# Combining matmuls cut into column tiles, and new positions for the steps around them, in a two-layer cross-attention and mixture-of-experts kernel

## The reference

```
x = x + cross_attention_0(layernorm(x), ctx)          # 16 heads of 8, all 1601 keys
x = x + experts_0(layernorm(x))                       # top 2 of 9, inner width 352
x = x + cross_attention_1(layernorm(x), ctx, indices) # 16 heads of 8, 64 chosen keys per query
x = x + experts_1(layernorm(x))                       # top 2 of 8, and a shared one, inner width 176
```

## Time and profile before

| | us |
|---|---|
| median of 3 runs | 1537.95 |
| lowest, highest | 1526.84, 1542.74 |
| the profiled execution's own time | 1533.95 |
| its span, first to last instruction | 1531.8 |
| PE, DVE, ACT, POOL busy | 1395.9, 1092.1, 789.7, 828.1 |

### The profile page before, as it was taken

One profiled execution on the slowest core, in us unless ns is written; L12 is line 12 of the kernel. 1 busy time (PEld: TensorE's weight loads), 2 busy tenths in 40 slices (PEclk: granted clock), 3 DMA queues, 4 the chain that ended last, 5 costly groups with the idle time before them and its releaser, 6 DMA issues.

```text
span 1531.8 us, 34069 instructions
## 1 busy us (share of the span) xinstructions
PE 1395.9 (91%) x12588; PEld 804.0 (52%) x12588; DVE 1092.1 (71%) x2283; ACT 789.7 (52%) x1200; POOL 828.1 (54%) x1381
## 2 busy tenths in 40 slices
PE   4899799999999999999999999999999999997987
PEld 2244464357533674347743575346843477334845
DVE  4885578866787668877688667876588776865663
ACT  3457337652575426772376524764266723773451
POOL 4356346755566545664457544675456644544462
PEclk8799899999998999999999999999999999997997
DMA  4505310132102330023201421023300331000111
GB/s 111 144 22 150 81 48 12 30 100 66 34 19 49 90 82 2 22 78 86 55 2 34 96 74 36 12 67 79 83 2 23 77 89 26 1 7 28 41 41 45
DMA packets 97654, 82.12 MB, mean 54 GB/s; under 512 B 17658, under 2 KB 90644, under 8 KB 97492
## 3 DMA queue, kind: packets, MB, share of 16 engines
q1 hardware_dynamic: 96916, 78.72, 19.8%
q10 hardware_dynamic: 576, 1.23, 0.3%
HBM read 67.29 MB, written 12.61 MB: 52 GB/s over the span
## 4 chain that ended last, share of the span: by engine, by line
PE 63%; DVE 20%; ACT 5%; POOL 5%; issue 4%; DMA 1%; SPq 0%; ACTq 0%; POOLq 0%; DVEq 0%
PE ob L788 10%; PE um L846 8%; PE ob L863 7%; DVE mx L1259 7%; PE um L847 7%; PE um L773 6%; PE um L758 6%; PE um L736 4%; ACT probs L1054 2%; DVE mx L1376 2%; DVE big L1372 2%; DVE xn L1157 2%; PE um L830 2%; PE um L913 2%; PE um L730 1%
## 5 line engine op out<-in xcount | busy, mean ns | idle before, releaser
L1259 DVE TENSOR_REDUCE mx<-um 128x2 f32<-128x802 f32 (+1 forms) x512 | 501.6, 989 | 177.3 <-PE um L758 173.6
L1054 ACT ACTIVATE probs<-um 128x1024 f32<-128x1024 f32 (+1 forms) x448 | 425.7, 963 | 215.2 <-PE um L773 211.0
L1452 POOL TENSOR_TENSOR hid<-hid,cwb 128x256 f32<-128x256 f32 (+1 forms) x304 | 217.0, 732 | 265.3 <-DVE hid L1271 130.2
L1060 ACT ACTIVATE hid<-um 128x256 f32<-128x256 f32 (+1 forms) x304 | 116.7, 384 | 346.0 <-PE um L847 336.8
L1458 POOL TENSOR_TENSOR big<-iotab,idx_lo 128x512 bf16<-128x512 bf16 x256 | 272.0, 1078 | 28.3 <-PE um L953 20.4
L788 PE MATMUL ob<-probs,vaug 128*9 128x256 f32 (+1 forms) x3328 | 280.6, 386 | 3.2 <-ACT oT L1035 2.7
L758 PE MATMUL um<-kst,qa 64*128 64x401 bf16 (+1 forms) x1024 | 178.4, 347 | 25.3 <-DMA kst<-k_parts 9.8
L773 PE MATMUL um<-big,kst 64*128 64x256 bf16 (+1 forms) x1664 | 171.1, 280 | 14.5 <-DVE mx L1376 4.8
L1271 DVE TENSOR_TENSOR hid<-hid,um 128x256 f32<-128x256 f32 (+1 forms) x304 | 124.4, 414 | 55.8 <-ACT hid L1060 53.0
L846 PE MATMUL um<-xnT,w1T 128*128 128x256 f32 (+1 forms) x400 | 129.3, 406 | 0.0
L863 PE MATMUL ob<-w2T,hid 128*128 128x128 f32 (+1 forms) x800 | 124.2, 280 | 4.6 <-POOL hid L1452 3.7
(11 more groups left out here) (221 smaller groups left out, 2087.9 us busy)
## 6 DMA issues: line engine op xcount, KB each, us to landing
kst<-k_parts SPq DMA_DIRECT2D x360, 50.0 KB
cwb<-cw_rows SPq DMA_DIRECT2D x112, 128.0 KB, 3.4
k_parts<-big SPq DMA_DIRECT2D x72, 128.0 KB, 1.9
ctx_sb<-in_ctx SPq DMA_DIRECT2D x7, 768.0 KB
cwb<-cw_rows SPq DMA_DIRECT2D x48, 96.0 KB, 3.0
k1st<-k_parts SPq DMA_DIRECT2D x96, 32.0 KB
cwb<-cw_rows SPq DMA_DIRECT2D x48, 64.0 KB, 2.7
cwb<-cw_rows SPq DMA_DIRECT2D x16, 112.0 KB, 3.0
```

The lines of the kernel that those rows point to most:

```text
L1054: act.activation(probs[0:kn, k:k + 2, 0:w], own_banks, ACT.Exp).then_inc(f_read, 1)
L1060: act.activation(hid[0:nr, own % NHID, :], quarter[place[ev][0]][0:nr, 0:NQ], ACT.Silu).then_inc(th_ready, 1)
L1259: dve.tensor_reduce(mx[:, p % 2, s, :, j], pair[:, :, 0:w], AX, ALU.max, negate=True).then_inc(u_read, 1)
L1452: pool.tensor_tensor(h, h, cwb[0:nr, k, :], ALU.mult).then_inc(hw_ready, 1)
```

## The change

Each half of 128 queries is combined in four products of 32 queries. The stationary operand is 32 columns of oT, the output goes to partitions 32t to 32t + 31, and the product stands in the column tile of that position. The numbers computed are the same. The positions change too: 42 of the 123 constants of AT, and SHIFT has 142 entries where it had 19.

```diff
             def combine(bank, o):
 
                 for s in range(NS):
-                    m = pe.matmul(bank[:, s * 2 * V1:(s + 1) * 2 * V1], o[:, s * P:(s + 1) * P], comb[:, :], start=True, stop=True)
+                    for t in range(P // QD):
+                        m = pe.matmul(bank[QD * t:QD * (t + 1), s * 2 * V1:(s + 1) * 2 * V1], o[:, s * P + QD * t:s * P + QD * (t + 1)],
+                                      comb[:, :], start=True, stop=True, tile_position=(0, QD * t))
                 return m
```

Of the tables AT and SHIFT, some of the entries that differ:

```diff
-'c0': 2.45,
+'c0': 2.488,
...
-'msk': 5.445,
+'msk': 3.549,
...
-'z_kv1': 29.559,
+'z_kv1': 25.056,
...
+('c1', 0): 0.456,
```

More of the change, by code:

```diff
@@ L63 @@
 MMAX = 512
-AT = {'cl': 0.75, 'cl1': 0.712, 'y1': -0.194, 'y0': 0.0, 'turn': 2.741, 'early': 32, 'first': 8, 'side': 1, 'p0': 1.03, 'p0s': 1.139, 'pf': -2.842, 'pfs': 0.697, 'px': -0.045, 'pxs': 1.201, 'psn': 6.134, 'ldx': 6.705, 'ldc': 2, 'ctx': 1.722, 'ctxs': 3, 'key': 20.43, 'keys': 5.896, 'val': 1.841, 'vals': 1.977, 'rel': 46.109, 'rel3': 7.976, 'n4': 35.264, 'n4a': 37.737, 'xT4': 40.416, 'pq0': 45.686, 'idx': 53.412, 'lat': 14.631, 'all0': 50.235, 'all0s': 0.854, 'q00': -0.617, 'q0': -3.597, 'w0': 2.361, 'ev0': 1.123, 'c0': 2.45, 'dfs': 1.5, 'df': 0.6, 'eq': 3.407, 'cnt': 5.833, 'kk1': 47.116, 'kv1': 48.342, 'nm0': 2.517, 'aT0': 3.214, 'o0': 4.015, 'n1': 4.1, 'n1a': 5.081, 'xT1': 6.202, 'gate0': 6.258, 'le0': 7.981, 'rt0': 8.969, 'msk': 5.445, 'mq': 12.77, 'hd': 0.663, 'n2': 0.43, 'n2a': 1.906, 'xT2': 2.481, 'pq1': 3.678, 'all1': 6.973, 'pair0': 8.803, 'pair': 4.232, 'pairl': 1.336, 'pair1': -0.133, 'q1': 1.982, 's1': 3.149, 'mu': 3.717, 'w1': 4.923, 'c1': 6.247, 'nm1': 47.2, 'aT1': 48.3, 'o1': 48.455, 'n3': 49.3, 'n3a': 50.296, 'xT3': 51.126, 'gate1': 52.618, 'le1': 53.007, 'rt1': 53.285, 'ct0': 10.321, 'ct1': 56.388, 'cm': 1.4, 'dk0': 3.2, 'dk1': 4.2, 'cl0': 2.0, 'cl1n': 1.651, 'b_ctx': 3.028, 'b_key': 1.5, 'b_val': -37.284, 'b_n4': -49.5, 'b_n4a': -47.678, 'b_xT4': -47.547, 'b_pq0': -46.6, 'b_all0': -37.556, 'b_ldw': 2.2, 'b_ldw2': 33.683, 'b_idx': -29.495, 'b_lat': -36.0, 'b_w1': 23.127, 'b_w1s': 1.95, 'b_sq': 36.0, 'b_w2': 42.939, 'b_w2s': 1.387, 'b_part': -20.0, 'b_pre': -46.9, 'b_ldc1': -31.95, 'z_rel1': 25.333, 'z_kv1': 29.559, 'z_mq': 30.079, 'z_pair0': -6.339, 'z_pair': 3.0, 'z_back': -24.258, 'z_chunk': 0.422, 'z_each': 0.489}
@@ L65 @@
-SHIFT = {('cnt', 11): -0.621, ('part', 44): 0.293, ('part', 45): 0.198, ('part', 26): -0.337, ('cnt', 14): -0.483, ('df', 28): -0.156, ('df', 7): 0.309, ('df', 8): 0.309, ('w1', 1): -0.211, ('pair1', 7): 0.319, ('part', 3): -0.1, ('part', 57): -0.306, ('key', 3): -0.019, ('cnt', 12): -0.118, ('mu', 2): -0.526, ('dk', 25): -0.13, ('eq', 6): -0.334, ('eq', 14): 0.727, ('c0', 6): 0.325}
+AT = {'cl': 0.75, 'cl1': 0.712, 'y1': -0.194, 'y0': 0.0, 'turn': 2.741, 'early': 32, 'first': 8, 'side': 1, 'p0': 1.03, 'p0s': 1.139, 'pf': -2.842, 'pfs': 0.697, 'px': -0.106, 'pxs': 1.201, 'psn': 6.134, 'ldx': 6.703, 'ldc': -1.841, 'ctx': 1.722, 'ctxs': 3, 'key': 20.43, 'keys': 5.896, 'val': 1.841, 'vals': 2.03, 'rel': 46.112, 'rel3': 7.976, 'n4': 35.955, 'n4a': 37.462, 'xT4': 40.416, 'pq0': 45.686, 'idx': 53.412, 'lat': 14.631, 'all0': 50.235, 'all0s': 0.818, 'q00': -0.617, 'q0': -3.597, 'w0': 2.361, 'ev0': 1.123, 'c0': 2.488, 'dfs': 1.5, 'df': 0.6, 'eq': 3.407, 'cnt': 5.833, 'kk1': 47.116, 'kv1': 48.342, 'nm0': 2.517, 'aT0': 3.214, 'o0': 3.951, 'n1': 4.1, 'n1a': 5.081, 'xT1': 6.01, 'gate0': 6.258, 'le0': 7.981, 'rt0': 8.969, 'msk': 3.549, 'mq': 12.707, 'hd': 0.663, 'n2': 0.43, 'n2a': 2.035, 'xT2': 2.481, 'pq1': 3.678, 'all1': 6.909, 'pair0': 8.803, 'pair': 4.232, 'pairl': 1.336, 'pair1': -0.133, 'q1': 1.982, 's1': 3.149, 'mu': 3.744, 'w1': 4.923, 'c1': 6.247, 'nm1': 47.2, 'aT1': 48.3, 'o1': 48.409, 'n3': 48.936, 'n3a': 50.169, 'xT3': 51.126, 'gate1': 52.618, 'le1': 53.007, 'rt1': 53.277, 'ct0': 10.233, 'ct1': 56.388, 'cm': 1.4, 'dk0': 3.2, 'dk1': 4.2, 'cl0': 2.097, 'cl1n': 1.651, 'b_ctx': 2.829, 'b_key': 0.893, 'b_val': -38.126, 'b_n4': -50.448, 'b_n4a': -48.263, 'b_xT4': -47.751, 'b_pq0': -46.376, 'b_all0': -37.106, 'b_ldw': 2.2, 'b_ldw2': 33.697, 'b_idx': -29.683, 'b_lat': -36.0, 'b_w1': 23.082, 'b_w1s': 1.95, 'b_sq': 36.134, 'b_w2': 42.939, 'b_w2s': 1.387, 'b_part': -20.661, 'b_pre': -47.253, 'b_ldc1': -31.908, 'z_rel1': 25.482, 'z_kv1': 25.056, 'z_mq': 30.079, 'z_pair0': -6.389, 'z_pair': 2.973, 'z_back': -24.131, 'z_chunk': 0.568, 'z_each': 0.489}
```

1 line of the change is left out of this document (added).

## The result

The changed kernel took 1509.45 us in the median (four runs, 1504.83 to 1517.33), the kernel before 1536.12 us beside it (four runs, 1526.84 to 1542.74): ratio 0.985, 95% interval 0.9808 to 0.9891. The forecast was 1511.0 us. The profiled execution took 1509.38 us with a span of 1507.3, against 1533.95 and 1531.8 before.

A forecast was written before the change was run, and what follows sets the result against it. PE was taken to set the pace. Cheaper combines (34.6 us) and fewer tiling changes (3.1) gave 37.7 us of PE time, times 0.86 and 0.85 is 27 us: 1511 us in the median, range 1494 to 1533.

The forecast's parts named there:

- The price of a combine before: On PE's queue, four 128-column loads 0.11 us apart: 0.44 us per uncut combine, 128 combines in the trace.
- Term 1: The cut combine on PE: column tiles load side by side, 0.17 us instead of 0.44, saving 34.6 us of PE time.
- Term 2: Changes of tiling between neighbours on PE's queue: 1917 fall to 1889, 28 x 0.11 = 3.1 us saved.
- The sign on busy time: Matmuls of the combine on PE: together busy under 35 us instead of 78.8 if the forecast is right.
- Term 3: Steps moved by the new position constants and shifts, on PE and DVE: costed at nothing.
- the mask step's 3 us: Mask step 1.9 slots earlier on DVE: 0.41 us x 8 = 3 us if idle time does not cover it.
- From PE time to the end: Of 37.7 us PE time, 0.86 on the chain and a further 0.85 after waits: 27 us reach the end.
- PE gives way to the waits: Rival: half the PE gain returns as waits for xn, DVE's products and maxima; 16 us gained, 1522 us; chance 0.12.
- The period: Distance between like steps of two steady batches: 177.0 us before, about 173.7 after.
- A fixed price of 25 ns per pass: Rival: each load with its pass costs 0.025 us, a cut combine 0.40 us; 1532 us; chance 0.16.
- an issue rate of 62 ns: Rival: PE's sequencer sustains one load per 62 ns, a cut combine costs 1.0 us; 1597 us; chance 0.05.
- loads that wait for the pass before: Rival: four rounds of 0.27 us in a tile make a cut combine 1.1 us; 1610 us; chance 0.01.

## Why the prediction was right, and which of its terms were off

**What bounds the kernel.** PE sets the pace as read from the earlier trace rows. When PE's busy time grew by some 72 us, the time grew by 58.

**The price of a combine before, 0.44 us.** Right: doubling it added 0.446.

**Term 1.** Right in its mechanism; at its own place a combine is cheaper than was taken. A combine takes 0.15 us from pass to pass (0.12 from load to load), not the 0.17 taken, so it sits at the lower end, 0.13. Four tiles load side by side, and a tile's next 32-column load follows after about 0.03 us. Behind a weighted sum 1.09 us became 0.66, which is 0.11 for the change of tiling and 0.32 for the combine, 0.44 to 0.12. Times 128 that would be 41 us, and 44 with Term 2. The trace as a whole does not show so much: with the missing records PE's busy time fell by some 30 us where 37.7 were forecast, and by some 34 if half of the 7.2 us more at the lower clock is added (an estimate). Why the sum is smaller than its parts stays open.

**The sign on busy time.** "Together busy under 35 us" was missed with 42.1. The step left out the tail: the union of sixteen passes is their 0.14 us of starts and the 0.19 us of the last one.

**Term 2.** That a like tiling saves a change holds: 0.12 us to a like neighbour, 0.25 to another (0.13 for the change instead of 0.11), and the tiles of 64, which match neither side, had a change on both (0.90 us for 0.66). The count of 28 was not tried by itself.

**Term 3, the moved steps at nothing.** Right for the sum, wrong as a statement about positions. With the cut combine they are worth 0.26%, which the intervals don't separate from zero (10 us between the medians); with the uncut one they cost 0.9%. The recorded counts are off as well: in the kernels 43 of 114 constants of AT differ, and SHIFT has 123 new entries and 5 changed ones. "Nothing" holds only for this one pairing, and the range for it should have come from a slower clock and a wait for POOL, not from the mask step's 3 us.

**From PE time to the end.** Factor 0.73 (0.86 x 0.85) was taken. By the page's rows it would be 24.5 / 40.1 = 0.61, with PE's idle time up by 15.6 us, over the 10 at which the prediction called its last step wrong. That reading rests on the 57 missing records. With them it is 24.5 / 30.3 = 0.81, with 6 us more idle time; the doubled uncut combine gives 58 / 72, the same. So the two errors go opposite ways: less PE time saved than forecast (30 for 37.7), more of it at the end (0.81 for 0.73). That 27 us were forecast and 24.5 measured in the profiled execution, 26.7 between the medians, is in part luck. The rival "PE gives way to the waits" had 0.43 and is out for the change as a whole. The share depends on the tables, though: with the old ones it is 14.9 us of span for some 34 of PE time, 0.43, in an execution with 10.5 us of waits for the routing weights' product; with the new ones 36.1 for some 46, 0.78. The prediction looked for the new waits at xn and DVE. The largest is POOL's (11.6 us more), which the earlier trace rows did not show since it was only 5.0 before; others became shorter (the one for DVE's products 12.7 to 9.3 us), so the idle time in all grew by less. The lower clock came with it.

**The period.** Seven like waits for xn, one per batch, lie 1075.0 us apart before (226.3 to 1301.3) and 1054.2 after (227.8 to 1282.0): 3.5 us less for each of six batches, against 3.3 predicted. The prediction gave a single pair of steps, 177.0 us before and about 173.7 after; that pair is 177.2 us after (753.10 to 930.3), and only the mean bears the forecast out, since single periods vary, 174.3 to 177.3 us. Of the other signs, L737 is not among the lines with 1% or more of the chain.

**The rivals.** A fixed price of 25 ns per pass, an issue rate of 62 ns and loads that wait for the pass before are all excluded by sixteen passes whose starts lie within 0.136 us (645.511 to 645.647), and by 8 ns for each of the doubled ones. The Trainium skill's rule that a load overlaps running matmuls only in another row group (TensorE: Matmul & The Clock Gate, Part 3, The mechanism) does not hold here: all four tiles have the same rows, and the combine's loads begin at 672.03 us while the weighted sum's matmuls, by their modelled ends, run until 672.43.

## What to carry to other kernels

Where a short product stands between others in column tiles, cut it into tiles of the same size: the loads go side by side, and a change of tiling goes as well; tiles of another size cost 26 us more here. Before a busy time is compared between two traces, compare the counts of matmuls and loads: 57 missing records made 10 us of idle time that was not there. When the bounding engine gets faster, look not only at its long waits of before but at each producer whose result came just in time, and at what that producer's queue holds ahead of it. Tables of positions are measured anew with every change of a duration: the same table was neutral or better with one combine and 0.9% slower with the other, and one small hold on POOL gave another 1%.

## What the runs showed of the hardware

- DVE's application of the normalisation (128x128, float32, one scalar pair) takes 0.33 to 0.35 us alone and 1.06 to 1.08 us beside a POOL TENSOR_TENSOR of 128x512 bf16. It was so for 14 of 64 before, and undoing it where it held PE up gave about 1% (ratio 0.9743 instead of 0.985, each against the kernel before).
- Most falls of the granted clock in the steady part stand at waits of PE of 1.4 us or more, and last 3.4, 6.8 or 10.2 us; not every such wait has one (9 of 13 in the changed kernel, 4 of 7 before). Filling one such wait moved the fall to the other (37.4 us against 40.8), removing one alone left 27.2 to 34.0 us, removing both left 3.4, each in one execution.
- The 10.2 us falls of the uncut combine with the new tables remained when PE's wait of 1.42 us beside them had become 0.43. Their cause is open.
- In column tiles, 32-column float32 loads with 18-column passes follow each other every 8 to 9 ns, in either order of the tiles; eight with 64 columns take 0.227 us, 28 ns each.
